# Attention softmax denominators: reciprocals stored to a DRAM scratch one number at a time, instead of transposed on the tensor engine first

## The chip, the cores and the metric

One NeuronCore of one Trainium2 chip. The metric is the device time of one execution in microseconds, the median of the runs.

## What is computed

One transformer block on 16 × 512 tokens of 128 features: a layer norm, then attention and a routed feed-forward on the normalised rows, both added to x.

```
xn = _layernorm(x)
h = _rmsnorm(xn, norm_scale);  q, k, v = h @ wq, h @ wk, h @ wv      # 16 heads of 64
weights = softmax(q k^T / 8);  attn = (weights @ v) @ w_out + b_out
logits = silu(xn @ rw1 + rb1) @ rw2 + rb2;  top 2 of 8 experts, softmax of the two
ffn = sum over the two of p_e * (silu(xn @ w1[e] + b1[e]) @ w2[e] + b2[e])
x + attn + ffn
```

What matters here is the softmax's denominator: each query row's sum of exponentials has to divide that row's result.

## The kernel before

The work is a row of 256 groups (`group(G)`, L947); two groups are one **pair** n, which is two heads of one batch element: 16 batches of 8 pairs, 128 pairs. T = 8192 tokens, S = 512 tokens per batch, QT = 4 tiles of 128 query rows. Each function adds instructions to a queue per engine; within a group the vector engine's and the scalar engine's instructions are sorted by `place` (DVE_ORDER and ACT_ORDER, L31 and L32, everything else being "side", last), while TensorE and SyncE keep the order in which they were added. Every engine runs its queue strictly in order, and waits at the head of it. In the code `needs` are the names of what an instruction waits for.

For pair n:

- `project` (L200 to L202, L334, L335) makes q and k, each split in a high and a low fp32r part. In the groups 2n and 2n+1 `scores` (L349) multiplies two of the four query tiles each, for both heads, into a PSUM pair, `maxima` (L355, DVE) takes the row maxima, and `probs` (L360, ACT) the exponentials into PR with their row sums in RS[128 rows, head, tile].
- `turn_probs` (L372) transposes the exponentials on TensorE, and DVE (L384) or ACT (L382) copies them to PT.
- `denominators` (L405, L406) takes the reciprocal of the 128×8 sums on DVE, in group 2n+2, at the place "inverse", between the first PT copies and the second maxima.
- `spread` (L409 to L420), in the same group 2n+2: the reciprocals lie one query per partition, but the result of the attention lies with queries along the free axis. So TensorE transposes RI [128×8] into a PSUM bank (L411), DVE copies the 8×128 numbers to RT (L413, place "side"), SyncE stores RT to the DRAM scratch l_rows (L416, 8 rows of 512 B), and, when that has landed, loads it back as RB [128×512] (L418), each head's row of 512 numbers repeated on 64 partitions. l_rows, RI, RT and RB have two buffers each, taken in turn by n.
- `weighted` (L395, L401) multiplies PT by V on TensorE at the end of group 2n+3, 16 matmuls; DVE then multiplies the bank by RB into OT (L401). That is the one place where RB is used. Ahead of the next group's maxima, DVE has to be through with it.
- `project_out` (L427, L428) multiplies two pairs' OT by w_out, in the even groups of every second pair, ahead of `spread` in TensorE's queue. `finish` (L445 to L457) turns a batch's sum.

Four PSUM banks (4 to 7) go round for all small results: `xbank()` (L174) hands out the next, and its new user waits for the copy that emptied the one before (`freed`). The transpose of the reciprocals takes one of them.

Beside this, in the first half (groups 0 to 127) run the router (L200 to L202 with `XT,R1`; L483 to L519), the choice of two experts (L547 to L587), the splitting of expert weights, and the scatter of rows to the experts' slots by GpSimd (L592). From group 138 on `experts` takes 39 tiles of 512 routed rows, three groups each: transpose (L678), three-product matmuls (L200 and L720 to L722), ACT and DVE work on the hidden layer (L698 to L712), and the return (L737, L741, L751, which adds rows to the output by GpSimd's indirect DMA).

In SyncE's queue, what `attending` adds in a group (loads of x, stores) stands ahead of `spread`; the router's loads, the weights' splitting, and the experts' loads stand behind it.

Of the kernel before, what the change touches and what calls it, by code (L numbers as in the profile page):

```python
# [15 lines left out]
P = 128  # L16
# [5 lines left out]
QT = S // P  # L22
# [14 lines left out]
class Queues:  # L37
# [7 lines left out]
    def add(self, engine, make, needs=(), name=None, step=1, sem=None, place="side"):  # L45
        key = None
        if name is not None:
            key = sem or (engine + "_" + name[0])
            self.count.setdefault(key, 0)
        self.open[engine].append((place, make, [n for n in needs if n is not None], name, key, step))  # L50
# [23 lines left out]
def block_kernel(nc, x, wq, wk, wv, wout, ns, bout, rw1, rb1, rw2, rb2, w1, w2, bias, ident, tri, consts, pick, out):  # L74
# [9 lines left out]
    q = Queues()  # L84
    add = q.add
    with ExitStack() as ctx:
        def sb(name, shape, dt=F32, to=ctx):
            return to.enter_context(nc.sbuf_tensor(name, shape, dt))

        xin = sb("xin", [P, 3, QT, D])  # L90
        idn = sb("idn", [P, P])
# [29 lines left out]
        junk = sb("junk", [1, 4])  # L121
        RS = sb("RS", [P, 2, 2, QT])
        RI = sb("RI", [P, 2, 2, QT])
        RT = sb("RT", [2 * QT, 2, P])
        RB = sb("RB", [P, 2, S])
        OT = sb("OT", [P, 4, S])
        acc = sb("acc", [P, QT, D])
# [35 lines left out]
        l_rows = nc.dram_tensor("l_rows", (2, 2 * QT, P), F32, kind="Internal").ap()  # L163
# [5 lines left out]
        bank = [pairs[i // 2][:, i % 2, :] for i in range(4)]  # L169
        bank += [ctx.enter_context(nc.psum_tensor(f"bank{i}", [P, 512], F32))[:] for i in range(4, 8)]  # L170
        freed = {}
        turn = [0]

        def xbank():  # L174
            turn[0] += 1
            return 4 + turn[0] % 4
# [227 lines left out]

        def denominators(n):  # L405
            add("dve", lambda e: e.reciprocal(RI[:, n % 2], RS[:, n % 2]),  # L406
                needs=[("exp", n, QT - 1, 1), ("R", n - 2) if n >= 2 else None], name=("ri", n), place="inverse")

        def spread(n):  # L409
            bk = xbank()  # L410
            add("pe", lambda e: e.transpose(bank[bk][0:2 * QT, 0:P], RI[:, n % 2].rearrange("p h t -> p (h t)"), idn[:]),  # L411
                needs=[("ri", n), freed.get(bk)], name=("R", n))
            add("dve", lambda e: e.tensor_copy(RT[:, n % 2, :], bank[bk][0:2 * QT, 0:P]),  # L413
                needs=[("R", n), ("rrow", n - 2) if n >= 2 else None], name=("rt", n))
            freed[bk] = ("rt", n)
            add("sp", lambda e: e.dma_start(l_rows[n % 2], RT[:, n % 2, :]), needs=[("rt", n), ("RB", n - 2) if n >= 2 else None],  # L416
                name=("rrow", n), step=16, sem=f"rrow_{n % 2}")
            add("sp", lambda e: e.dma_start(RB[:, n % 2, :], l_rows[n % 2].rearrange("(h t) q -> h (t q)", h=2).unsqueeze(1)  # L418
                                            .to_broadcast([2, DH, S])),
                needs=[("rrow", n), ("OT", n - 2) if n >= 2 else None], name=("RB", n), step=16, sem=f"RB_{n % 2}")  # L420
# [368 lines left out]
        for k in range(WARM):  # L789
            add("pe", lambda e: e.matmul(bank[7][:, 0:256], PR[:, 7, 0:P], PR[:, 7, 0:256], start=True, stop=True),  # L790
                needs=[("ones",)], name=("warm",))
# [8 lines left out]
        for key in (True, False):  # L800
# [12 lines left out]
            needs=[("pad0",)], name=("pad",))  # L813
# [133 lines left out]
        def group(G):  # L947
# [16 lines left out]
            if G % 2 == 0 and 1 <= G <= GROUPS:  # L964
                denominators(G // 2 - 1)
            halves_after(G)
            attending(G)
            if G % 2 == 0 and 1 <= G <= GROUPS:
                spread(G // 2 - 1)
# [85 lines left out]
```

How the kernel before makes its waits and increments, by code:

```python
    def emit(self, engine, eng, sems):  # L62
        seen = {}
        for make, needs, key, step in self.items[engine]:
            for sem, value in (self.value[n] for n in needs):
                if seen.get(sem, 0) < value:
                    eng.wait_ge(sems[sem], value)
                    seen[sem] = value
            ins = make(eng)
            if key is not None:
                ins.then_inc(sems[key], step)
# [915 lines left out]
        @block.sync  # L987
        def _(eng):
            q.emit("sp", eng, sems)
            for k, v in q.count.items():
                if k.startswith(("st_", "sadd", "spare_out", "base", "rrow", "tab", "b_tab", "sc_", "pads")):
                    eng.wait_ge(sems[k], v)
```

## Time and profile before

| | |
|---|---|
| median of 3 runs (lowest, highest) | 2347.66 us (2343.93, 2350.57) |
| the profiled execution's own time | 2347.15 us |
| its span in the trace | 2345.3 us |
| PE busy | 2199.6 us, 94%, 12720 matmuls |
| DVE busy | 1752.8 us, 75%, 2908 instructions |
| ACT busy | 1453.1 us, 62%, 3455 |
| POOL busy | 952.1 us, 41%, 793 |
| DMA | mean 60 GB/s; 16 engines; 16.2% of them taken by SyncE's queue |
| chain that ended last, by engine | PE 47%, DVE 21%, DMA 12%, ACT 9%, issue 7% |
| in it, by line | PE L395 14%, PE L349 10%, DMA RB<-l_rows 9%, PE L372 8%, DVE L355 7%, DMA l_rows<-RT 2% |

PE is the tensor engine's matmuls, PEld its weight loads, DVE VectorE, ACT ScalarE, POOL GpSimd, SPq SyncE's queue of DMA issues. "Busy" is the time covered by instructions, whose ends on PE are modelled: two matmuls in a row overlap in the records, so the distance between two starts tells what one costs. "The chain that ended last" is followed back from the last instruction, at each step to what released it. "Idle before" is the time in which an engine stood still ahead of an instruction, with what ended it.

### The profile page before, as it was taken

How to read it: one execution, taken by the hardware profiler on the slowest of the kernel's cores; microseconds unless marked ns; L12 is line 12 of the kernel's file. 1: busy time of each engine (PE TensorE's matmuls, PEld its weight loads, DVE VectorE, ACT ScalarE, POOL GpSimd, SP SyncE). 2: the span in 40 equal slices, each digit the busy share in tenths (PEclk: the TensorE clock that was granted, in tenths of full speed). 3: DMA queues.
4: the chain of work that ended last, by engine and by line, in shares of the span. 5: the costliest groups of instructions: out<-in, count | busy, mean ns of one | idle time of the engine just before them, and what ended most of it. 6: DMA issues, size and time to landing. Idle time of an engine off the chain costs nothing.

```text
span 2345.3 us, 36846 instructions
## 1 busy us (share of the span) xinstructions
PE 2199.6 (94%) x12720; PEld 1395.6 (60%) x12720; DVE 1752.8 (75%) x2908; ACT 1453.1 (62%) x3455; POOL 952.1 (41%) x793
## 2 busy tenths in 40 slices
PE   8999999999999999997999998999989989999997
PEld 5666566656666666654656665565656655656654
DVE  6777777777778878775777776777767767777775
ACT  5666666666666666654665665666666656666663
POOL 5333343544343433310145445445454354454353
PEclk8999999999999999998999999999999999999999
DMA  2122222211111010003133333323233223232232
GB/s 73 34 64 78 85 80 82 91 46 34 37 37 35 27 42 33 29 31 89 37 69 73 73 70 59 71 69 76 69 72 73 59 56 73 69 73 69 66 67 46
DMA packets 126856, 141.67 MB, mean 60 GB/s; under 512 B 18480, under 2 KB 93104, under 8 KB 126640
## 3 DMA queue, kind: packets, MB, share of 16 engines
q1 hardware_dynamic: 96080, 118.60, 16.2%
q0 software_dynamic: 30592, 20.73, 7.2%
q8 instruction: 102, 1.67, 0.3%
q14 instruction: 82, 0.67, 0.1%
HBM read 102.92 MB, written 38.46 MB: 60 GB/s over the span
## 4 chain that ended last, share of the span: by engine, by line
PE 47%; DVE 21%; DMA 12%; ACT 9%; issue 7%; POOL 2%; DVEq 0%; SPq 0%; ACTq 0%; POOLq 0%
PE bank L395 14%; PE pair L349 10%; DMA RB<-l_rows 9%; PE bank L372 8%; DVE NM L355 7%; DVE PT L384 3%; ACT PR L360 3%; DVE ZZ L709 2%; PE bank L427 2%; PE bank L428 2%; PE bank L200 2%; DMA l_rows<-RT 2%; ACT PT L382 2%; PE bank L720 2%; DVE QS L335 1%
## 5 line engine op out<-in xcount | busy, mean ns | idle before, releaser
L360 ACT ACTIVATE PR<-pair,NM 128x512 f32<-128x512 f32 x1024 | 715.0, 706 | 707.5 <-DVE NM L355 706.3
L355 DVE TENSOR_REDUCE NM<-pair 128x2 f32<-128x1024 f32 x512 | 617.3, 1206 | 135.2 <-PE pair L349 134.8
L372 PE MATMUL bank<-idn,PR 128*128 128x128 f32 x4096 | 560.7, 279 | 34.8 <-DVE PT L384 16.6
L372 PEld LDWEIGHTS bank<-idn,PR 128*128 128x128 f32 x4096 | 460.2, 142 | 181.5 <-issue 86.0
L395 PE MATMUL bank<-PT,V 128*64 128x512 f32 x2048 | 469.4, 600 | 15.4 <-ACT ZZ L700 8.7
L712 POOL TENSOR_TENSOR HH<-ZZ,HH 128x512 fp32r<-128x512 f32 x156 | 231.7, 1494 | 572.2 <-DVE HH L711 572.2
L349 PE MATMUL pair<-KS,QS 64*128 64x512 f32 x3072 | 435.6, 415 | 2.1 <-DVE QS L335 1.1
L349 PEld LDWEIGHTS pair<-KS,QS 64*128 64x128 f32 x3072 | 273.8, 187 | 190.1 <-issue 137.1
L384 DVE COPY PT<-bank 128x512 f32<-128x512 f32 x512 | 349.9, 683 | 18.5 <-PE bank L372 10.8
L382 ACT COPY PT<-bank 128x512 f32<-128x512 f32 x512 | 302.9, 592 | 8.5 <-PE bank L372 8.5
L395 PEld LDWEIGHTS bank<-PT,V 128*64 128x64 f32 x2048 | 136.2, 137 | 276.7 <-issue 230.6
L751 POOL DMA_INDIRECT out<-YS,IDW x156 | 245.0, 1571 | 71.1 <-issue 34.2
L489 POOL TENSOR_TENSOR TH<-TH,HS 128x512 f32<-128x512 f32 x64 | 82.2, 1285 | 460.0 <-ACT HS L486 459.7
L401 DVE TENSOR_TENSOR OT<-bank,RB 128x512 f32<-128x512 f32 x128 | 88.1, 688 | 239.9 <-PE bank L395 156.5
L360 ACT ACTIVATION_READ_ACCUMULATOR PR<-pair,NM 128x1 f32 x1024 | 221.7, 216 | 0.0
L592 POOL DMA_INDIRECT slots<-XR,IDX x128 | 124.7, 974 | 106.1 <-DVE junk L587 71.8
L709 DVE SCALAR_TENSOR_TENSOR ZZ<-ZT,ZZ 128x512 f32<-128x512 f32 x156 | 107.2, 687 | 76.6 <-ACT ZZ L700 76.4
L698 ACT ACTIVATE ZT<-bank,BT 128x512 f32<-128x512 f32 x156 | 110.6, 709 | 56.3 <-POOL HH L712 53.3
L711 DVE CAST HH<-ZZ 128x512 fp32r<-128x512 f32 x156 | 138.0, 884 | 5.4
L700 ACT ACTIVATE ZZ<-bank,BT 128x512 f32<-128x512 f32 x156 | 111.0, 711 | 0.0
L335 DVE TENSOR_TENSOR QS<-bank,QS 128x512 fp32r<-128x512 f32 x128 | 88.5, 691 | 16.3 <-ACT QS L334 13.9
L335 DVE TENSOR_TENSOR KS<-bank,KS 128x512 fp32r<-128x512 f32 x128 | 87.7, 685 | 14.8 <-ACT KS L334 14.4
(164 smaller groups left out, 2866.4 us busy)
## 6 DMA issues: line engine op xcount, KB each, us to landing
E<-w_tab SPq DMA_DIRECT2D x78, 512.0 KB, 7.3
RB<-l_rows SPq DMA_DIRECT2D x128, 256.0 KB
XG<-slots SPq DMA_DIRECT2D x39, 264.0 KB, 7.4
w_tab<-SPL SPq DMA_DIRECT2D x16, 512.0 KB, 4.8
xin<-in_x SPq DMA_DIRECT2D x16, 256.0 KB, 7.7
XQ<-in_x SPq DMA_DIRECT2D x16, 256.0 KB, 6.9
RAW<-in_w SPq DMA_DIRECT2D x16, 256.0 KB, 7.9
slots<-PAD SPq DMA_DIRECT2D x15, 264.0 KB, 5.1
```

The source lines that it names most:

```text
L335: add("dve", lambda e: e.tensor_tensor(lo, bank[bk], hi, ALU.subtract), needs=[(name + "hi", n), *old], name=(name + "lo", n), place="low")
L349: m = e.matmul(bank[bk + j], a[half[j], cols], c[half[j], :], start=(k == 0), stop=(k == 2))
L355: add("dve", lambda e: e.tensor_reduce(NM[:, 2 * t:2 * t + 2], pairs[t % 2][:], AX.X, ALU.max, negate=True), needs=[("S", n, t), ("exp", n ...
L360: add("act", lambda e: e.activation(PR[:, k, :], bank[t % 2 * 2 + j], ACT.Exp, bias=NM[:, k:k + 1], accum_out=RS[:, n % 2, j, t:t + 1]), n ...
L372: m = e.transpose(bank[bk][:, c * P:(c + 1) * P], PR[:, k, c * P:(c + 1) * P], idn[:])
L382: add("act", lambda e: e.copy(dst, src), needs=[("T", n, t, j), *old], name=("PT", n, t, j), place=f"turn{t % 2}")
L384: add("dve", lambda e: e.tensor_copy(dst, src), needs=[("T", n, t, j), *old], name=("PT", n, t, j), place=f"turn{t % 2}")
L395: m = e.matmul(bank[bk][j * DH:(j + 1) * DH, :], V[:, k, h * DH:(h + 1) * DH], PT[:, n % 2 * 2 + j, k, :], start=(k == 0), stop=(k == QT - 1))
L709: add("dve", lambda e: e.scalar_tensor_tensor(ZZ[:, r], ZT[:, r], 1.0, ZZ[:, r], ALU.add, ALU.mult), needs=[("zt", n), ("zz", n)], name=(" ...
L711: add("dve", lambda e: e.tensor_copy(hi, ZZ[:, r]), needs=[("s", n), old], name=("hi", n))
L712: add("pool", lambda e: e.tensor_tensor(lo, ZZ[:, r], hi, ALU.subtract), needs=[("hi", n), old], name=("lo", n))
L751: add("pool", lambda e, t=t: e.indirect_dma_start(out, bass.IndirectOffsetOnAxis(ap=IDW[:, i % 4, t, 0:1].bitcast(U32), axis=0), YS[:, i % ...
```

## The change

The transpose of the reciprocals (L411), the bank it took, its copy (L413) and the tile RT go. SyncE's DMA reads RI [128 partitions × 8] and writes each number to its own place in l_rows (row r, query q, 4 bytes; the eight numbers of one partition go to places 512 B apart). It waits for the reciprocal; the reciprocal of pair n, which overwrites RI's buffer, waits for the store of pair n−2 where it waited for the transpose. The load of RB is the same.

```diff
-        RT = sb("RT", [2 * QT, 2, P])
...
         def denominators(n):
             add("dve", lambda e: e.reciprocal(RI[:, n % 2], RS[:, n % 2]),
-                needs=[("exp", n, QT - 1, 1), ("R", n - 2) if n >= 2 else None], name=("ri", n), place="inverse")
+                needs=[("exp", n, QT - 1, 1), ("rrow", n - 2) if n >= 2 else None], name=("ri", n), place="inverse")
 
         def spread(n):
-            bk = xbank()
-            add("pe", lambda e: e.transpose(bank[bk][0:2 * QT, 0:P], RI[:, n % 2].rearrange("p h t -> p (h t)"), idn[:]),
-                needs=[("ri", n), freed.get(bk)], name=("R", n))
-            add("dve", lambda e: e.tensor_copy(RT[:, n % 2, :], bank[bk][0:2 * QT, 0:P]),
-                needs=[("R", n), ("rrow", n - 2) if n >= 2 else None], name=("rt", n))
-            freed[bk] = ("rt", n)
-            add("sp", lambda e: e.dma_start(l_rows[n % 2], RT[:, n % 2, :]), needs=[("rt", n), ("RB", n - 2) if n >= 2 else None],
-                name=("rrow", n), step=16, sem=f"rrow_{n % 2}")
+            add("sp", lambda e: e.dma_start(l_rows[n % 2].rearrange("r q -> q r"), RI[:, n % 2].rearrange("p h t -> p (h t)"),
+                                            allow_slow_non_contiguous=True),
+                needs=[("ri", n), ("RB", n - 2) if n >= 2 else None], name=("rrow", n), step=16, sem=f"rrow_{n % 2}")
             add("sp", lambda e: e.dma_start(RB[:, n % 2, :], l_rows[n % 2].rearrange("(h t) q -> h (t q)", h=2).unsqueeze(1)
                                             .to_broadcast([2, DH, S])),
                 needs=[("rrow", n), ("OT", n - 2) if n >= 2 else None], name=("RB", n), step=16, sem=f"RB_{n % 2}")
```

## Rows read from the trace of the kernel before

**Rows 1.** Windows: stretch, its length, busy us (instructions) per engine, PEclk, DMA share, GB/s.
```profile
220.00:520.00 300.00, 291.78 (x1760) 180.80 (x1760) 233.43 (x457) 196.05 (x483) 136.14 (x128) 1.00 0.24 76
...
1400.00:1700.00 300.00, 278.01 (x1564) 178.91 (x1563) 223.81 (x312) 187.63 (x430) 136.43 (x100) 0.99 0.31 70
```

**Rows 2.** Waits from 40 to 1030 us: who waited for whom, us in total, times, longest.
```profile
DVE OT L401 <- DMA RB<-l_rows: 61.1, 34, 3.9
```

**Rows 3.** Timeline from 704 to 719 us, pair 42: start, us, instruction, [idle before, its releaser].
```profile
704.93 0.19 DVE L406 RECIPROCAL RI<-RS 128x8 f32<-128x8 f32 x1
...
708.71 0.27 DVE L413 COPY RT<-bank 8x128 f32<-8x128 f32 x1
...
709.01 0.29 SPq L416 DMA_DIRECT2D l_rows<-RT  x1
710.23 0.51 SPq L418 DMA_DIRECT2D RB<-l_rows  x1
...
717.79 0.69 DVE L401 TENSOR_TENSOR OT<-bank,RB 128x512 f32<-128x512 f32 x1 [1.24 <-DMA RB<-l_rows]
```

**Rows 4.** Timeline of PE (L395) and DVE (L401): pairs 16 and 17, 40 and 41.
```profile
300.96 3.65 PE L395 MATMUL bank<-PT,V 128*64 128x512 f32 x16
...
304.98 0.69 DVE L401 TENSOR_TENSOR OT<-bank,RB 128x512 f32<-128x512 f32 x1 [1.40 <-DMA RB<-l_rows]
...
316.40 3.65 PE L395 MATMUL bank<-PT,V 128*64 128x512 f32 x16
...
682.00 3.65 PE L395 MATMUL bank<-PT,V 128*64 128x512 f32 x16
...
687.02 0.69 DVE L401 TENSOR_TENSOR OT<-bank,RB 128x512 f32<-128x512 f32 x1 [1.43 <-DMA RB<-l_rows]
...
698.46 3.65 PE L395 MATMUL bank<-PT,V 128*64 128x512 f32 x16
```

**Rows 5.** Timeline of DVE: the first and the last of the 34 waits for RB.
```profile
50.21 0.69 DVE L401 TENSOR_TENSOR OT<-bank,RB 128x512 f32<-128x512 f32 x1 [1.26 <-DMA RB<-l_rows]
...
1001.69 0.69 DVE L401 TENSOR_TENSOR OT<-bank,RB 128x512 f32<-128x512 f32 x1 [3.12 <-DMA RB<-l_rows]
```

**Rows 6.** DMA view of 41.2:42.5 (one L416) and of 112:114.5 (the store b_tab).
```profile
DMA packets 16, 0.00 MB, mean 3 GB/s; under 512 B 8, under 2 KB 16, under 8 KB 16
...
q1 hardware_dynamic: 1044, 0.07, 24.2%
...
b_tab<-BIN SPq DMA_DIRECT2D x1, 64.0 KB, 2.2
```

**Rows 7.** Waits from 1030 us to the end.
```profile
DVE OT L401 <- DMA RB<-l_rows: 22.3, 5, 8.5
PE bank L737 <- DVE V L317: 22.3, 9, 2.5
```

**Rows 8.** The chain that ended last, 1590:1620, by line; then a piece of 2305:2346.
```profile
by line: PE bank L395 24.1%; PE pair L349 15.9%; issue 7.6%; PE bank L372 7.4%; DVE NM L355 7.1%; DVE PT L384 6.6%; DVE ZZ L709 4.4%; PE bank L720 3.9%; PE bank L721 3.1%; PE bank L722 3.1%; DVE V L317 2.3%; DVE KS L335 2.3%; PE bank L737 2
...
2327.01 7.86 DMA RB<-l_rows
```

**Rows 9.** Timeline of PE around the transpose L411, in pairs 42 and 43.
```profile
707.84 0.27 PE L411 MATMUL bank<-idn,RI 128*8 128x128 f32 x1
707.95 0.96 PE L515 MATMUL bank<-PICK,LG 128*128 128x8 f32 x8
...
722.74 0.40 PE L202 MATMUL bank<-WV,HT 128*128 128x512 f32 x1
722.98 0.27 PE L411 MATMUL bank<-idn,RI 128*8 128x128 f32 x1
...
723.61 0.39 PE L201 MATMUL bank<-XT,R 128*128 128x512 f32 x1
723.84 0.40 PE L202 MATMUL bank<-XT,R 128*128 128x512 f32 x1
...
724.30 0.39 PE L201 MATMUL bank<-XT,R 128*128 128x512 f32 x1
```

## The prediction, made before the changed kernel ran

> **What bounds the kernel now.** First the table of windows [rows 1]: in the first half (220 to 520 us) TensorE is busy 291.8 of 300 us at a granted clock of 1.00, its upper level of 2.4 GHz, so its clock is not in play; in the second half (1400 to 1700) it is busy 278.0 of 300 us, and DVE 223.8. TensorE's own list of work sets the pace, strictly in the first half, mostly in the second; what it loses, it loses to other engines being late. Then the waits, for who is late [rows 2]: DVE, at the multiplication by RB (L401), stands still 61.1 us in 34 waits because RB has not landed. That is the work around this change.
>
> The timeline of pair 42 [rows 3] shows the way of a reciprocal. It is ready at 705.12 (704.93 plus 0.19). Its transpose stands late in TensorE's queue and its copy late in DVE's, so the copy only starts at 708.71 and ends at 708.98; the store is issued at 709.01, lands before the load is issued at 710.23 (1.2 us), and the load takes until just before 717.79, about 7.5 us. So 3.9 of the 12.7 us from reciprocal to product go to the detour over TensorE and DVE, and of these only some 0.4 us are work on it: the rest is waiting in line.
>
> Is a late RB paid for in full? I compare two pairs of one place in the batch's rhythm [rows 4]. Pair 16: the 16 matmuls L395 end at 304.61, the product starts at 304.98, 0.37 late; the next pair's L395 starts 15.44 us after this one's. Pair 40: 685.65, 687.02, 1.37 late; the next starts 16.46 us after. One us more of lateness, 1.02 us more of period: the maxima stand behind the product in DVE's queue, and everything behind the maxima. This also says that only the lateness beyond the matmuls counts, not the whole idle time (1.40 and 1.43 us). Taken in the same way over the 34 waits, it comes to 31 us, the first and the last at 50.21 and 1001.69 [rows 5].
>
> **The change part by part**, against the profiled execution's own 2347.15 us (span 2345.3); the median is 0.5 us above that, which is nothing here.
>
> 1. *The store is issued earlier.* SyncE mostly has nothing else at its head when it waits here, so the issue moves from 709.01 to about 705.15, 3.9 us earlier in this pair; in pair 43 the transpose comes a little sooner, and 3.4 us is the middle of the first half.
>
> 2. *The store is of 1024 numbers instead of 8 rows.* Before, 16 packets went (8 of data) and it landed in 1.2 us. The trace has no store of single numbers. The nearest row is b_tab [rows 6]: the same 1024 pieces by the same queue from 128 partitions, each of 64 B to scattered places. Its packets took 24.2% of 16 engines for 2.5 us, 9.7 us in all for 1044 packets, 9.3 ns each, 64 per engine or 0.6 us; it landed in 2.2 us. Bounds: 1.2 us (no dearer than now) below; above the load of RB, 7.5 us, the slowest landing in these rows, which moves 64 times the bytes [rows 3]. I take 2.2 us, since the count of packets is the same and a smaller piece is no more work for the engine. Then RB lands 3.4 − 1.0 = 2.4 us earlier in an ordinary pair.
> The Trainium skill (DMA: Bandwidth & Descriptors, Rules for kernel authors) speaks against the change: a non-contiguous last dimension becomes one descriptor per element, and should be rearranged away. By the row on b_tab that costs 1.0 us here and not more; no row shows it for 4 B.
>
> 3. *Lateness.* With RB 2.4 us earlier nearly all of the 31 us of lateness is gone, as the single cases are 0.37 and 1.37 us. Some periods have slack of another kind (a pair whose next work is late anyway), so I take 27, with 15 and 31 as ends. What is late next is L395 itself, so DVE waits for TensorE, which is free.
> From 1030 us on, 22.3 us are waited in 5 waits [rows 7], 8.5 of them in the very last pair. The four others, 13.8 us, lie where the experts start; I take a quarter, 3 us. The last pair keeps its wait: the reciprocal to copy is 0.7 us there, the store's extra 1.0 us takes it back, and behind it stands the load of 7.86 us [rows 8]. Zero.
>
> 4. *TensorE loses 128 transposes.* The distance between starts tells the cost [rows 9]. In even pairs (42) the transpose stands between two fp32 products: 707.84 to 707.95, 0.11 us. In odd pairs with the router behind it (43), L202 at 722.74 to the next but one L201 at 723.61 is 0.87 us; the same steps without a transpose between them, L202 at 723.84 to L201 at 724.30, take 0.46. So 0.4 us, as the change of kind costs on both sides. 24 pairs are of this sort; for the other 104 I take 0.11: 24 × 0.4 + 104 × 0.11 = 21 us. All of it is on the path where TensorE is the pace. Ends: none of it (0), and 128 × 0.4 = 51.
>
> 5. *DVE loses 128 copies* of 0.27 us [rows 3], 35 us. In the first half it is hidden, as DVE waits for TensorE once RB is in time. In the second half the chain is DVE's for about a quarter of its length [rows 8]: 64 × 0.27 × 0.23 = 4 us. Ends 0 and 17.
>
> 6. *One user fewer of the four banks.* Every result behind it then takes a bank that was given out one step earlier, so no wait for a bank can get longer. L737 waits 22.3 us in 9 waits for DVE's copy of V [rows 7], whose bank it would no longer get. But the product behind it (L741) stands in DVE's own full queue, so I take 2 us; ends 0 and 22.
>
> 7. *The new wait of the reciprocal* for the store of pair n−2 is 30 us old by then: nothing. RI is read by the DMA instead of TensorE, the same buffer rule.
>
> Sum: 27 + 3 + 21 + 4 + 2 = 57 us; 2347.15 − 57 = **2290 us**.
>
> **The rivals.**
>
> *A. The scattered store is slow, and RB comes later than before.* Place: between L416 and L418 on SyncE. Break-even on lateness is a landing of 1.2 + 3.4 = 4.6 us; about 34 to 61 of the first half's pairs then pay each further us, say 45. The 27 us of parts 4 to 6 are used up 0.6 us later, so it decides from a landing of 5.2 us on, that is (5.2 − 1.2) / 64 = 62 ns per packet against 9.3 measured. At 8 us: 3.4 × 45 = 153 us of new lateness less 27: about 2475 us. For it: 16 numbers from four or more engines share each 64 B of the scratch, which no row shows. Against: the packets' 9 ns, and the 2.2 us of b_tab. Chance 0.11. The Trainium skill (DMA: Bandwidth & Descriptors, Specifications) says that below 512 B the DMA reads, modifies and writes; b_tab's 64 B pieces are below that too and landed in 2.2 us, so by that row the rule costs the 1.0 us already counted.
>
> *B. The store takes back just what the detour cost* (landing 4 to 5 us). Lateness stays, parts 4 to 6 remain: 2347 − 27 = 2320 us. Chance 0.10.
>
> *C. The lateness goes, TensorE's transposes give nothing*, since another engine sets the pace as soon as that one is quicker: 2347 − 30 = 2317 us. For it: the first half's share of idle TensorE is small, but ACT and DVE have chains of their own through each pair. Against: the transposes stand among matmuls at full pace [rows 9]. Chance 0.12.
>
> *D. Nothing to be measured*: the lateness moves to another wait, the DMA load of RB runs into other transfers at its new time. Chance 0.03. That the change does not do what it says I leave out: the order of the queues gives the earlier issue by itself.
>
> The forecast keeps 0.64.
>
> **How the numbers follow.** Predicted is the likeliest, 2290. Within the forecast the ends of parts 3 to 6 reach to about 2265 (all lateness, TensorE 30, DVE and banks 20) and 2315. B and C lie at 2320 and 2317. A range of 2266 to 2333 holds about 0.6 of the forecast's 0.64 and most of B and C, 0.8 in all. A difference of 0.3% (7 us) is about what a measurement of this kernel can tell from none. Faster by more: forecast, C and B less a little, 0.84. Slower: A, 0.11. Same: D and the borders of A and B, 0.05.
>
> **What would show it.** The store's issue within 0.1 us of the reciprocal's end, and RB's issue 2.2 us behind it: longer than 4.6 us means A or B. DVE's waits for RB before 1030 us below 5 us in total, instead of 61.1. Starts of L395 in pairs 16 and 17, and 40 and 41, at equal distances of about 15.1 us, the same for both: if they are equal but still 15.17 or more, C. TensorE's instructions fewer by 128, and L202 to L200 in odd pairs 0.23 us. In the second half, periods shorter by some tenths of a us. Wrong it would be if the store's packets took over 60 ns, or if other transfers stretched RB's 7.5 us.

## The result, and the profile after

The changed kernel takes 2886.13 us (2880.26 to 2886.58, 4 runs) against 2349.01 us of the kernel before: a ratio of 1.228 (95% interval 1.2262 to 1.2298), 537 us more. The forecast was 2290 us, 2266 to 2333.

First the windows of the changed kernel, for [rows 1]; columns as there.

```profile
220.00:520.00 300.00, 240.99 (x1276) 148.60 (x1272) 164.14 (x314) 140.80 (x346) 95.26 (x90) 0.88 0.22 60
...
1400.00:1700.00 300.00, 242.72 (x1291) 150.24 (x1288) 177.80 (x269) 147.16 (x350) 74.07 (x58) 0.91 0.29 53
```

In the same 300 us TensorE starts 1276 matmuls instead of 1760, and 1291 instead of 1564. It is busy 241 us instead of 292 in the first stretch, and its granted clock, 1.00 before, is 0.88 there, a mean between its two levels. Something else has become the bound. The chain of waits from the changed kernel's page says what:

```profile
DMA 78%; DVE 10%; issue 6%; PE 3%; POOL 2%; ACT 1%; DVEq 0%; SPq 0%; ACTq 0%; POOLq 0%
DMA l_rows<-RI 42%; DMA RB<-l_rows 34%; DVE NM L354 5%; DVE PT L383 3%; DMA out<-YS,IDW 1%; PE bank L394 1%; POOL out L456 1%; POOL out L745 1%; PE pair L348 1%; DVE RI L405 1%; POOL HH L706 0%; DMA out<-xin,TOK 0%; PE bank L371 0%; ACT PR L359 0%; DVE ZZ L703 0%
```

The chain was 47% TensorE and 12% DMA; now 78% of it is DMA, 42% the scattered store alone. The waits of the changed kernel (whole span; the second row is of SyncE's queue), for [rows 2, 7]:

```profile
DVE OT L400 <- DMA RB<-l_rows: 741.8, 123, 17.3
...
SPq L412 <- DMA l_rows<-RI: 1269.1, 123, 12.4
```

DVE's product (now L400) waits for RB in 123 of 128 pairs, not in 39. SyncE waits 10.3 us on average (1269.1 / 123) between the store and the load (L412); before, it was about 1.

Pair 42 again, from the changed kernel's timeline, for [rows 3]:

```profile
965.52 0.19 DVE L405 RECIPROCAL RI<-RS 128x8 f32<-128x8 f32 x1
...
965.74 0.36 SPq L409 DMA_DIRECT2D l_rows<-RI  x1
...
977.58 0.51 SPq L412 DMA_DIRECT2D RB<-l_rows  x1
...
984.47 0.69 DVE L400 TENSOR_TENSOR OT<-bank,RB 128x512 f32<-128x512 f32 x1 [6.42 <-DMA RB<-l_rows]
```

The store is issued 0.03 us behind the reciprocal's end: the detour is gone as meant, 3.9 us won. But the store needs 11.8 us to land where it had needed 1.2. From reciprocal to product it is 18.8 us instead of 12.7. The view of the DMA engines between the store's issue and the load's, 965.7 to 977.6 us (digits: busy tenths of 40 slices of 0.3 us), shows where in these 11.8 us the work is, for [rows 6]:

```profile
DMA  0005720000000000000000000000000000000000
...
DMA packets 1040, 0.00 MB, mean 0 GB/s; under 512 B 1040, under 2 KB 1040, under 8 KB 1040
...
q1 hardware_dynamic: 1040, 0.00, 3.9%
```

1024 of the packets are the numbers. They took 3.9% of 16 engines for 11.9 us, 7.4 us in all or 7 ns each, less than the 9.3 ns I had reckoned, and all were through within two us of the issue. Then no packet moves for ten us, and SyncE still waits. I read it so that the writes have been sent and are not confirmed; the trace shows only that the time lies behind the last packet.

### The profile page after: what moved, and what is told of

Same layout as the page of the kernel before. It is cut to its first block, busy times and chain, and to the rows that moved or that the text cites. A ratio compares the mean times of both kernels' runs of the same rounds, so it can differ in the third digit from the quotient of the medians.

```text
span 2884.0 us, 36333 instructions
## 1 busy us (share of the span) xinstructions
PE 2376.6 (82%) x12592; PEld 1482.5 (51%) x12592; DVE 1708.5 (59%) x2780; ACT 1456.0 (50%) x3455; POOL 952.5 (33%) x793
## 4 chain that ended last, share of the span: by engine, by line
DMA 78%; DVE 10%; issue 6%; PE 3%; POOL 2%; ACT 1%; DVEq 0%; SPq 0%; ACTq 0%; POOLq 0%
DMA l_rows<-RI 42%; DMA RB<-l_rows 34%; DVE NM L354 5%; DVE PT L383 3%; DMA out<-YS,IDW 1%; PE bank L394 1%; POOL out L456 1%; POOL out L745 1%; PE pair L348 1%; DVE RI L405 1%; POOL HH L706 0%; DMA out<-xin,TOK 0%; PE bank L371 0%; ACT PR L359 0%; DVE ZZ L703 0%
## 5 line engine op out<-in xcount | busy, mean ns | idle before, releaser
L371 PE MATMUL bank<-idn,PR 128*128 128x128 f32 x4096 | 629.6, 294 | 393.1 <-DVE OT L400 251.4
L371 PEld LDWEIGHTS bank<-idn,PR 128*128 128x128 f32 x4096 | 474.9, 148 | 600.5 <-DVE OT L400 288.8
L400 DVE TENSOR_TENSOR OT<-bank,RB 128x512 f32<-128x512 f32 x128 | 88.5, 691 | 758.7 <-DMA RB<-l_rows 741.8
L348 PEld LDWEIGHTS pair<-KS,QS 64*128 64x128 f32 x3072 | 279.8, 191 | 195.4 <-issue 139.5
L421 PE MATMUL bank<-OT,WO 128*128 128x512 f32 x128 | 98.5, 863 | 15.1 <-DVE OT L400 13.0
```

Source lines behind the costliest of these rows:

```text
L348: m = e.matmul(bank[bk + j], a[half[j], cols], c[half[j], :], start=(k == 0), stop=(k == 2))
L371: m = e.transpose(bank[bk][:, c * P:(c + 1) * P], PR[:, k, c * P:(c + 1) * P], idn[:])
```

## The experiments

All ratios are to the kernel before on the same chip: 2345.38 us for e1, e2, e3 and e8; 2343.47 for e4, e9, e10 and e12; 2388.27 for e5, e6, e11 and e13; 2347.74 for e14, e15, e16 and the repeat of e12. Only e5, e11, e15 and the repeat of e12 have several runs and an interval; the others ran once, so small differences between them say nothing. "Store to load" is the median distance from the issue of the store to that of RB's load over the 128 pairs, read from SyncE's timeline; it is 1.2 us before, 11.1 us in the changed kernel. In all variants but e1, e4, e5, e6, e8 and e11 the load of RB reads a scratch of ones (l_ones), in the same shape and behind the same wait, so that the store's places can be changed freely; these variants leave out the division by the sums, and e1 multiplies by the reciprocals in a wrong order.

### What makes the store slow

Three theories: the number of single-number writes (C), their sharing a short stretch of DRAM (L), or all of them falling in one place (P).

**e1**: one piece of 32 B per partition.

```diff
-            add("sp", lambda e: e.dma_start(l_rows[n % 2].rearrange("r q -> q r"), ...
+            add("sp", lambda e: e.dma_start(l_rows[n % 2].rearrange("r q -> (r q)").rearrange("(q r) -> q r", r=2 * QT), ...
```

> The changed kernel, but the eight reciprocals of a partition go side by side, 32 B in one piece, 128 pieces instead of 1024 (RB then multiplies by the numbers in a wrong order). In the changed kernel the load's issue followed the store's by 11 us. Theory C (count: every single-number write costs the memory some 8 to 9 ns one after another): 128 pieces, load's issue about 2.3 us behind the store's. Theory L (line: 16 numbers share each 64 B, and such writes wait for each other): two pieces share 64 B, about 2 us. Both give a total near my forecast, 2285 to 2310 us; if the total stays above 2340 with the store at 2 us, the parts of the forecast about the tensor engine and the lateness are wrong too.

2283.24 us, 0.974; store to load 1.44 us. Nothing is wrong with the rest of the change: with a quick store the kernel is 62 us below the one before, near the 57 that I had forecast for a store of 2.2 us.

**e2**: single numbers, 64 B apart.

```diff
-        l_rows = nc.dram_tensor("l_rows", (2, 2 * QT, P), F32, kind="Internal").ap()
+        l_rows = nc.dram_tensor("l_rows", (2, 2 * QT, P, 16), F32, kind="Internal").ap()
...
-            l_rows[n % 2].rearrange("r q -> q r")
+            l_rows[n % 2, :, :, 0].rearrange("r q -> q r")
```

> Still 1024 single numbers, but each in a 64 B stretch of its own (the scratch is 16 times as large); RB is loaded from a scratch of ones, in the same shape and after the same wait. Theory L: the issue of the load comes 2 to 2.5 us behind the store's, total 2280 to 2310 us. Theory C: still about 11 us, total about 2880 us. Theory P (place: all writes fall in one 4 KB stretch of DRAM): 2 to 4 us.

2294.25 us, 0.978; store to load 2.7 us. Two rows of its SyncE timeline:

```profile
377.08 0.37 SPq L410 DMA_DIRECT2D l_rows<-RI  x1
379.79 0.51 SPq L413 DMA_DIRECT2D RB<-l_ones  x1
```

The same 1024 packets of 4 B. Theory C is dead: 1024 single writes instead of 8 rows are worth 1.5 us, not 10.

**e3**: `l_rows` of shape (2, 8, 4096), of each row the first 128 numbers: the rows 16 KB apart.

> 1024 single numbers, 16 neighbours in each 64 B as in the changed kernel, but the eight rows lie 16 KB apart instead of 512 B; RB is loaded from a scratch of ones. Theory P: 2 to 5 us between the issues, total 2280 to 2350 us. Theories L and C: 10 to 12 us and about 2880 us.

4749.97 us, 2.03 times the kernel before; store to load 25.7 us.

```profile
1545.68 0.36 SPq L410 DMA_DIRECT2D l_rows<-RI  x1
1569.78 0.50 SPq L413 DMA_DIRECT2D RB<-l_ones  x1
```

Theory P said that spreading helps; this spreading more than doubles the wait. None of the three had that.

**e10**: both together, `l_rows` of shape (2, 8, 256, 16), so that each number has 64 B and the rows lie 16 KB apart.

> 1024 single numbers, each in 64 B of its own, with the eight rows 16 KB apart. With shared stretches the 16 KB between rows took the wait from 11.1 to 25.7 us. If the distance matters only where writes share a stretch: 2.7 us and 2290 to 2300 us. If it matters by itself (rows of DRAM that are opened in turn): 5 us or more, total above 2350 us.

2289.48 us, 0.977; store to load 2.8 us. So the distance of 16 KB costs nothing by itself; it makes dearer what the sharing costs, and why it does is open. P is dead too.

**e12**: `l_rows` of shape (2, 8, 128, 4), numbers 16 B apart. **e9**: shape (2, 128, 8, 2), the eight numbers of a partition 8 B apart. **e13**: the same with the partitions 512 B apart, shape (2, 128, 64, 2).

> 1024 single numbers in the changed kernel's order, but 16 B apart, so that four neighbouring partitions share 64 B. Theory L: 2.7 + 3 x 0.56 = 4.4 us between the issues, total 2300 to 2330 us. If the stretch that counts is 32 B, two share it: 3.3 us. If what counts is the crowding of all writes in few KB (16 KB here, 64 KB with 64 B each, 4 KB in the changed kernel), the same about 4 us; e10 tells that apart.

> 1024 single numbers, the eight of one partition 8 B apart in a 64 B stretch that no other partition writes; RB from a scratch of ones. If every further write to a stretch of 64 B adds the same time (theory L in its plain form): between one to a stretch (2.7 us from the store's issue to the load's) and sixteen (11.1 us) there are 8.4 us for 15 writes, 0.56 us each; eight to a stretch gives 2.7 + 7 x 0.56 = 6.6 us, total about 2450 us. If only writes from different partitions (that is, different DMA engines) hinder each other: about 2.7 us and 2290 to 2300 us.

> As e9 (the eight numbers of a partition 8 B apart in one 64 B stretch), but the partitions' stretches lie 512 B apart instead of 64 B, so the scratch is eight times as thinly written. If sharing 64 B is what costs: 6.2 us between the issues as in e9, total 2395 to 2410 us. If what costs is how many writes fall in 512 B or in a few KB: 2.7 to 3.5 us, 2288 to 2295 us.

e12: 2291.22 us, 0.978, store to load 3.4 us; a second time, in four runs, 2295.63 us, 0.9775 (0.9759 to 0.9791). e9: 2403.81 us, 1.026, 6.2 us. e13: 2465.66 us on a chip where the kernel before took 2388.27, 1.032, 6.8 us. Two rows of e9:

```profile
875.17 0.56 SPq L410 DMA_DIRECT2D l_rows<-RI  x1
881.41 0.50 SPq L413 DMA_DIRECT2D RB<-l_ones  x1
```

e13 has one eighth of e9's writes in any 512 B and is no quicker, and it has as many writes in any 512 B as e2, which took 2.7 us; so it is the short stretch that counts. The eight that share a stretch come from one partition, so writes need not come from different ones to hinder each other. The distances read:

| single numbers in one 64 B stretch | store to load, us | run |
|---|---|---|
| 1 | 2.7, 2.8 | e2, e10 |
| 4 | 3.4 | e12 |
| 8 | 6.2, 6.8 | e9, e13 |
| 16 | 11.1 | the changed kernel |
| 16, rows 16 KB apart | 25.7 | e3 |

From 4 to 16 it goes by (11.1 − 3.4) / 12 = 0.64 us per further number on average, though not evenly: 0.2 us each from 1 to 4, 0.7 to 0.9 from 4 to 8, 0.5 to 0.6 from 8 to 16. The time goes with the number in one stretch and not with how many stretches there are (64 in the changed kernel, 128 in e9, 256 in e12, 1024 in e2). This fits stretches that work side by side, with the writes within one going one after another; that they do so is argued, not seen.

**e14** asked whether the stretch is 64 or 32 B, by two stores that write four numbers into one half of each 64 B, the other half unused:

```diff
+            for h in range(2):
+                add("sp", lambda e, h=h: e.dma_start(l_rows[n % 2, h, :, 0:QT, 0], RI[:, n % 2, h, :], allow_slow_non_contiguous=True), ...
```

> 1024 single numbers by two stores, one per head: the four numbers of a partition and head lie 8 B apart in the first 32 B of a 64 B stretch, the other half is unused. e9 had four in 32 B and eight in 64 B and took 6.2 us from store to load, e12 two in 32 B and four in 64 B and took 3.4. If 64 B is the shared stretch: 3.4 to 3.8 us and about 0.977 of before. If 32 B: 6.2 to 6.6 us and about 1.025.

2354.77 us, 1.003; store to load 5.3 us, between the two. Slower than the 3.4 us of e12, it speaks for 32 B (four of them there instead of two), but it has two stores instead of one, and their order within a DMA engine differs. e12 speaks for 32 B too: its 3.4 us is what I had expected of such a stretch (3.3), not of one of 64 B (4.4). Counted by 32 B, with 1, 2, 4 and 8 numbers, the steps are more even: 0.6 us for the second number, 1.4 to 1.7 each for the third and fourth (e9, e13), 1.2 each from there to eight. This stays open; a stretch of 32 B would make the mean price per number 1.3 us.

### What a slow store does to others

**e4**: the kernel before, and the scattered store beside it, to a scratch nobody reads.

```diff
+            add("sp", lambda e: e.dma_start(l_dummy[n % 2].rearrange("r q -> q r"), RI[:, n % 2].rearrange("p h t -> p (h t)"),
+                                            allow_slow_non_contiguous=True),
+                needs=[("ri", n), ("pads2", n - 2) if n >= 2 else None], name=("pads2", n), step=16, sem=f"padsd_{n % 2}")
```

> The kernel before, and beside its own store also the scattered store of the changed kernel, to a scratch that nobody reads and that only the reciprocal of two pairs later waits for. Theory W (the time is lost in waiting for the scattered store's landing): 2345 to 2360 us, within 0.7% of before. Theory T (the slow writes disturb other traffic, above all the load of RB that follows): RB lands later, total above 2400 us. SyncE's issue of it, 0.37 us, should cost nothing.

3170.59 us, 1.353: worse than the change itself. Theory W (time is lost only by waiting for the landing) had expected almost nothing, theory T more than 2400 us. One pair of its timeline, SyncE and then DVE:

```profile
812.42 0.30 SPq L417 DMA_DIRECT2D l_rows<-RT  x1
812.82 0.37 SPq L419 DMA_DIRECT2D l_dummy<-RI  x1
813.65 0.52 SPq L422 DMA_DIRECT2D RB<-l_rows  x1
...
828.50 0.69 DVE L402 TENSOR_TENSOR OT<-bank,RB 128x512 f32<-128x512 f32 x1 [8.71 <-DMA RB<-l_rows]
```

The kernel's own store lands as ever, in 1.2 us. The load of RB is issued 0.8 us behind the scattered one and is there after 14.8 us instead of 7.5. It is not stopped, but slow: the DMA engines move 16 GB/s from 817.0 to 824.5 us and 40 GB/s from there to 828.4 (in the kernel before, pair 42: 48 GB/s from 712.0 to 717.4). The pair whose scattered store is issued at 859.20 shows the same, 15 and then 40 GB/s, with the step near 870.9. Both steps lie about 11.7 us behind the scattered store's issue, about when such a store lands, so I take it that its unconfirmed writes hold the load up. Others are slow too; of its page's list of DMA issues (KB each, median us to landing):

```profile
E<-w_tab SPq DMA_DIRECT2D x78, 512.0 KB, 14.8
...
XG<-slots SPq DMA_DIRECT2D x39, 264.0 KB, 15.3
```

They took 7.3 and 7.4 us before. GpSimd's scatters of rows, on a queue of their own, took 3.3 us (before 2.3), and 3.3 us also in e16 below, which has no slow write; nothing shows that other queues are held up. So a slow write cannot be hidden by not waiting for it, as long as something that matters is issued behind it on the queue. In the changed kernel SyncE holds the load back until the store has landed, and the same loads take 7.8 and 7.6 us.

**e16**: is the whole loss the wait? e12 with six plain stores in a row put between its store and the load.

```diff
+            for d in range(6):
+                add("sp", lambda e: e.dma_start(l_tmp, ONES[0:2 * QT, :]), needs=[("tab_d", n, d - 1) if d else ("rrow", n)], ...
```

> e12 with six plain stores of 8 rows of 512 B in a row between its own store and the load, each waiting for the one before: 3.4 + 6 x 1.2 = about 10.7 us from the store to the load, near the changed kernel's 11.1, with no slow write in it. If the later issue of the load is all: ratio to before about 1.21 (changed kernel: 1.228). If a good part of the loss is that slow writes hold up what stands behind them on the DMA engines: 1.12 to 1.18.

2795.03 us, 1.191; store to load 10.7 us. Its matmuls of exponentials, beside those of the changed kernel, from the groups of instructions of e16 and then of the changed kernel:

```profile
L373 PE MATMUL bank<-idn,PR 128*128 128x128 f32 x4096 | 617.7, 290 | 344.5 <-DVE OT L402 204.3 <-DVE PT L385 118.9 <-ACT ZZ L699 11.4
```

```profile
L371 PE MATMUL bank<-idn,PR 128*128 128x128 f32 x4096 | 629.6, 294 | 393.1 <-DVE OT L400 251.4 <-DVE PT L383 121.7 <-ACT ZZ L694 10.8
```

The same picture with no slow write in it: TensorE stands still ahead of the transposes because DVE's product is late. A plain delay of this length gives 447 of the 537 us; the ratio of 1.191 lies between what I had expected if the delay were all (1.21) and if a good part were not (1.12 to 1.18). The other 90 fit what is left: 0.4 us more from store to load, and RB's load itself longer in the changed kernel (8.3 against 7.5 us in the first half, 8.5 against 7.9 in the second), 1.0 to 1.2 us in nearly every pair; over 128 pairs that is 150 us at most, and not every pair pays it whole. Why the load is longer was not tried.

### What the rest of the change is worth

**e15**: e12 with the transpose, its bank and its copy put back as dead work (nobody uses the copy).

```diff
+            bk = xbank()
+            add("pe", lambda e: e.transpose(bank[bk][0:2 * QT, 0:P], RI[:, n % 2].rearrange("p h t -> p (h t)"), idn[:]), ...
+            add("dve", lambda e: e.tensor_copy(RT[:, n % 2, :], bank[bk][0:2 * QT, 0:P]), needs=[("R", n)], name=("rt", n))
+            freed[bk] = ("rt", n)
```

> e12 with the transpose of the reciprocals, its bank and its copy put back as dead work: nobody waits for the copy. Forecast's parts 4 to 6: 27 us more than e12, ratio to before about 0.988. If the whole gain of e12 is the lateness: no more than 5 us above e12. If the three parts are worth what e5 leaves (e5 took 0.9%, e12 2.2%): about 35 us above e12, ratio 0.991 to 0.993.

> e12 again, with intervals, as the base for e15: ratio to the kernel before 0.977 (0.974 to 0.980).

2325.58 us, 0.9905 (0.9887 to 0.9922), against 2295.63 us and 0.9775 of e12 on the same chip: the three parts on TensorE, DVE and the banks are worth 30 us, between the 27 and the 35 expected. What e15 gains on the kernel before, 22 us, is the lateness alone, and not all of it: with a store of 3.3 us its product still waits for RB 10 times before 1030 us, 16.3 us in all, where it was 34 times and 61.1. Its waits from 1030 us on show one of the forecast's rows as it was, while in e12 the nine waits for V stand at the transposes L372, 7.8 us in all:

```profile
PE bank L739 <- DVE V L318: 22.2, 9, 2.5
```

**e5** and **e6**: the load of RB in two, into the kernel before and into the changed kernel.

```diff
+            for h in range(2):
+                add("sp", lambda e, h=h: e.dma_start(RB[h * DH:(h + 1) * DH, n % 2, :],
+                                                     l_rows[n % 2, h * QT:(h + 1) * QT].rearrange("t q -> (t q)").unsqueeze(0)
+                                                     .to_broadcast([DH, S])), ...
```

> The kernel before with the same two loads. The 31 us of lateness in the first half, some us at the start of the experts and about 5 us in the last pair go, the transposes and copies stay: 2345 - 31 - 3 - 5 = 2306 us (2295 to 2320). If it stays above 2335, the reading of the 34 waits was wrong.

> The changed kernel, with the load of RB as two DMAs, one per head, each of 64 partitions of one contiguous row, so that it can run on 16 DMA engines instead of the 2 that it seems to use. If so, the load takes 2.5 to 4 us instead of 8.3, and reciprocal to product 11.2 + 3.5 = 14.7 us instead of 19.5. The lateness of 5.8 us per pair in the first half falls to about 1: total 2380 to 2450 us instead of 2886.

e5: 2365.18 us against 2388.27, 0.9911 (0.9891 to 0.9932), 21 to 23 us less: the size of e15's gain, reached from the other end of the same chain, and well below the 39 I had expected. In the last pair RB is there 3.5 us after the load's first issue instead of 7.9. Before 1030 us no product waits for RB any more; this is e5's only row of the product's waits there:

```profile
DVE OT L401 <- PE bank L395: 76.0, 61, 2.8
```

The split also quickens loads that stand behind RB's on the queue: in e5 XG takes 4.2 us instead of 7.4, and xin 4.0 instead of 7.7. What part of e5's gain is theirs was not tried.

e6: 2573.48 us, 1.078, store to load still 11.7 us, load 4.1: of a loss of 22.8% two thirds are gone without touching the store, still less than I had expected (2380 to 2450).

Before, the load's packets took 12.4% of 16 engines from 711.5 to 717.6 us, the time of two engines; in e5 up to six tenths of the 16 are busy with them. That the load's first dimension of 2 had put it on two DMA engines is in keeping with the Trainium skill (DMA: Bandwidth & Descriptors, Rules for kernel authors), which says that an outermost dimension of c below 16 confines a DMA to at most c engines; here two of 64 took half the time of one of 2 × 64.

**e8**: a version that computes everything. A piece of 16 B per partition and head, and the product reads RB in the order query, tile.

```diff
-        l_rows = nc.dram_tensor("l_rows", (2, 2 * QT, P), F32, kind="Internal").ap()
+        l_rows = nc.dram_tensor("l_rows", (2, 2, P, QT), F32, kind="Internal").ap()
...
-            add("dve", lambda e: e.tensor_tensor(OT[:, n % 4, :], bank[bk], RB[:, n % 2, :], ALU.mult), ...
+            add("dve", lambda e: e.tensor_tensor(OT[:, n % 4, :].rearrange("p (t q) -> p t q", t=QT), bank[bk].rearrange(...),
+                                                 RB[:, n % 2, :].rearrange("p (q t) -> p t q", t=QT), ALU.mult), ...
```

> A version that computes everything: each partition's four reciprocals of a head go as one piece of 16 B (256 pieces), so the scratch is ordered head, query, tile; the load is as before, and the product reads RB with a step of four numbers. Theory C: 1.2 + 256 x 9 ns, about 3.5 us between the issues. Theory L: four pieces to 64 B, about 3 us. Total 2285 to 2320 us; the product may get longer than 0.69 us by its strided reading.

2300.81 us, 0.981; store to load 2.2 us. The product's group of instructions, 1.07 us instead of 0.69 with its strided reading:

```profile
L400 DVE TENSOR_TENSOR OT<-bank,RB 128x512 f32<-128x512 f32 x128 | 137.3, 1072 | 207.2 <-PE bank L394 191.5 <-DMA RB<-l_rows 15.4
```

**e11**: e8 with the load in two.

> e8 (complete, 16 B pieces, strided product) with the two loads. e8 took 2301 us; the last pair's wait of 10.3 us and the few others get shorter by 4 to 5 us each: 2288 to 2297 us. It should be the quickest complete version, though the product's 1.07 us costs DVE 0.38 us per pair.

2338.65 us against 2388.27, 0.9802 (0.9785 to 0.9819). That is 2.0% below the kernel before; on a chip where that one takes 2346 us it would be about 2300 us, where e8 alone was (0.981 in one run). The two are not told apart, and the 2288 to 2297 us expected of e11 were missed: the second step adds little once the first is done.

## Why the prediction was wrong

It was wrong at one step, **part 2**: "I take 2.2 us, since the count of packets is the same and a smaller piece is no more work for the engine." It measured 11.1 us. The reason is right and beside the point: the DMA engines took 7 ns per packet. The time runs after the last packet and is set by how many of the writes share a short stretch of DRAM. b_tab's pieces were 64 B each, so none shared one, and the row could not show the price. The upper bound of 7.5 us, from the load of RB, was a number without a mechanism and too low; the range did not use even that one to its end. The Trainium skill (DMA: Bandwidth & Descriptors, Specifications) says that a DMA below 512 B reads, modifies and writes. I had put that aside by b_tab. The measured steps of about 0.6 us for each further number in a stretch look like such round trips, one waiting for the other; that they are is argued, not shown. Of the forecast's two signs of a slow store one would have kept silent (over 60 ns a packet; it was 7), the other spoke (more than 4.6 us between the two issues).

**Part 1** held: issue 0.03 us behind the reciprocal, in the median 3.8 us earlier, 3.3 in the first half (3.4 forecast).

**Part 3**: RB 31 us late in sum, 27 + 3 forecast, and 22 measured (e15, with some waits left). e5, in which no product before 1030 us waits for RB, gained 21 to 23 us, of which some 5 lie in the last pair (a wait of 3.9 us instead of 8.5). The mechanism is right and the size at least a third too high; where the rest stayed was not tried.

**Parts 4 to 6**: 27 us forecast, 30 measured (e15 against e12, intervals of about ± 4 us each). How they share out between TensorE, DVE and the banks was not tried. The wait for V's bank did go from L737, as part 6 had it, but not from the kernel: of its 22.3 us in 9 waits, 7.8 us in 9 waits stand in e12 ahead of the transposes L372, where there had been none for V, against part 6's rule that no wait for a bank can get longer.

**Part 7** held: no wait of a reciprocal for a store is among the changed kernel's waits.

**The sum** of 57 us was thus 52 by measurement: e1, with a store that lands in 1.44 us, took 2283 us, and e2 and e12 2291 to 2296. Part 3 was too high and parts 4 to 6 a little low, so that the sum comes out closer than its terms. Had the store landed in the 2.2 us of part 2, the forecast would have stood.

**Rival A** is what happened, by the very ground that stood in its favour (16 numbers to 64 B), and I gave it 0.11. Its break-even of 5.2 us is borne out: e14 with 5.3 us lies at 1.003, e9 with 6.2 us at 1.026. Its price was too low: at 11.1 us it would give (11.1 − 4.6) × 45 − 27 = 265 us, not 537. It let 45 pairs of the first half pay; in the changed kernel all of the first 64 pairs and 59 of the last 64 wait for RB, where it had been 35 and 4. Nor is the price even: from e12 (3.3 us, 2296 us) to e14 (5.3 us, 2355 us) one us costs 59 / 2.0 = 30 us, from there to e16 (10.7 us, 2795 us) 440 / 5.4 = 81 us. And with TensorE waiting, its mean granted clock is 0.93 in e16 and 0.92 in the changed kernel, where it was 0.98, and its own work gets longer (a transpose of exponentials 294 ns instead of 279); how much of the loss that is was not separated. Rivals B, C and D did not occur; e15 and e12 speak directly against C.

## What to carry to other kernels

Before small values are stored one by one, look at how they lie in DRAM, not at how many they are: 1024 numbers, each in 64 B of its own, landed in 2.7 us, with sixteen to 64 B in 11.1 us, and as pieces of 16 or 32 B in 2.2 and 1.4 us. A row of the trace prices another transfer only if the two are alike at both ends, the far memory included; where no row is, the rival with a mechanism deserves more than a tenth. And look at the first dimension of a small broadcast load: cut in two, it took half the time, and other loads behind it got quicker too.

## What was not expected of the hardware

- 1024 single-number writes land the later the more of them share a short stretch of DRAM, by 0.64 us on average for each further one in 64 B (4, 8 and 16 of them: 3.4, 6.2 and 11.1 us), while the packets themselves take 7 ns. Whether the stretch is 64 or 32 B is open.
- With the eight rows 16 KB apart the same sharing costs 25.7 us; without sharing, 16 KB cost nothing (2.8 us).
- Transfers issued behind such a store on the same queue are slowed even when nothing waits for the store: loads that took 7.3 us took 14.8.
- A broadcast load of 256 KB cut in two shortened not only itself but loads behind it on the queue (XG 7.4 to 4.2 us).
- A 128×512 product on DVE whose second operand is read with a step of 16 B takes 1.07 us instead of 0.69.
